# Gathers with their row numbers read in place: a grouped MoE kernel on one Trainium2 core

## Chip, cores and metric

One core of a Trainium2 chip. The metric is device time in microseconds (us), median of several runs; lower is better. TensorE is PE in the profile (its weight loads PEld), VectorE is DVE, ScalarE is ACT, GpSimd is POOL, and SyncE is SP. SP computes nothing here: it issues the plain DMAs. POOL issues the indirect ones.

## The reference

```python
# x: 64 x 64 x 512, so 4096 tokens of 512 values; 8 adapters of rank 16; 2 shared and 16 routed experts, 512 -> 256 -> 512
c = x @ W.T + scal[a] * ((x @ A[a].T) @ Bm[a].T)          # a: the adapter of each batch of 64 tokens
shared = sum_e gelu(c @ Wsh_up[e]) @ Wsh_down[e]
probs = softmax(c @ W_router); top_v, top_i = top_k(probs, 2)
routed = sum over the token's 2 experts of top_v * (gelu(c @ Wrt_up[e]) @ Wrt_down[e])
out = x + shared + routed
```

## The kernel before, in words

The tokens go in 16 chunks of 256, that is two tiles of 128 tokens each. There are four stages.

1. **Conditioning.** For each chunk PE computes `c` and the router's logits, SP stores `c` by rows in `xc_dram` and transposed in `xcT_dram`. DVE and ACT split the fp32 weights and activations into two fp16 halves.
2. **Early shared experts and sorting.** Chunks 0 to 5 go through the shared experts. DVE sorts the (token, expert) pairs into tiles of 128 rows of one expert each: `tok[:, j]` holds the token numbers of tile `j`, 79 tiles in all, and `pos[:, r, n]` holds, for the tokens of tile `n`, where their `r`-th routed row will lie. Both are finished once; the semaphore `sorted_ready` says so. While DVE sorts, POOL does some of the elementwise work of this stage: `add_x` (L537, the residual x of a chunk), `low_condT` (L542) and `low_hid` (L547, the low fp16 half of what `shared_down`, L1340, multiplies).
3. **Routed experts.** For each of the 79 tiles, POOL gathers 128 rows of `xc_dram` into one of two buffers `xg` (the function `gather`, L566), PE transposes them (`r_transpose_x`, L1377), multiplies up (L1393), transposes the middle (L1402) and multiplies down (L1412), and ACT scales the result into `rrow`, which SP stores in `r_dram`. A gather of tile `j` waits until PE has transposed tile `j - 2` (`xgT_psum`).
4. **The rest.** PE takes chunks 6 to 15 through the shared experts, `shared_up` (L1327) of one chunk ahead of `shared_down` (L1340) of the chunk before it. For all 16 chunks the routed rows are gathered back from `r_dram` (`gather_back`, L594), four indirect DMAs of 128 rows for each chunk, and DVE adds them, weighted by `gate`, onto the chunk's sum (`weigh`, L1168). I call these groups L6 to L15 for the chunks whose shared part is done in this stage, and E0 to E5 for the early chunks, whose sums were stored in `s_dram` and are loaded again. For L-chunks DVE then adds the shared part out of PE's bank (`add_shared`, L1193), and `shared_down` of the next chunk waits for that bank. SP loads x, the transposed `c` and the early sums, and stores the sums to `out`.

The order of each engine's queue is written out by hand. In stage 4 POOL's order of groups is L6 L7 E0 E1 L8 L9 E2 L10 E3 L11 E4 L12 E5 L13 L14 L15. There are four buffers of four tiles each (`slot`), so from L8 on a group first waits until DVE has weighed the group that had its buffer: L15 waits for E5 (`e_weighed`), for example. DVE's order for chunk c from 8 to 13 is `add_shared(c-1)`, `low_condT(c+2)` (L1123), weigh E(c-8), `low_hid(c+1)` (L1161), weigh L(c). PE's order is up(c+1), down(c), up(c+2), down(c+1), and so on.

In front of each gather (stage 3) and of each group of four (stage 4) POOL copies the row numbers out of `tok` or `pos` into a small tile, `slot_idx` (L571) or `row_idx` (L603), and waits for that copy's semaphore before it issues the indirect DMA (L574, L608). Most of both sequences are hardware loops (`pool.Fori`), so the column of `tok` or `pos` is a register there; the copy brings it to a fixed address.

Of the kernel before, what the change touches and what calls it, by code (L numbers as in the profile page):

```python
# [8 lines left out]
I32 = mybir.dt.int32  # L9
U32 = mybir.dt.uint32  # L10
# [5 lines left out]
P = 128  # L16
# [41 lines left out]
def adaln_moe_kernel(nc, xT, x_rows, idx, WT, AT, BmT, scal, sh_up, sh_dn, rt_w, w_r, out):  # L58
# [17 lines left out]
    with ctx:  # L76
        def sb(name, shape, dt=F32):
            return ctx.enter_context(nc.sbuf_tensor(name, shape, dt))

        def sem(name):  # L80
            return ctx.enter_context(nc.semaphore(name))
# [156 lines left out]
        def col(v, n):  # L238
            return v[:, n:n + 1]

        slot_idx = [sb(f"slot_idx{s}", [P, 1], I32) for s in range(2)]
        row_idx = [sb(f"row_idx{s}", [P, K_TOP, NT], I32) for s in range(4)]

        bank = [ctx.enter_context(nc.psum_tensor(f"bank{i}", [P, 512], F32)) for i in range(8)]
        XA, COND, XPOSE, LOGIT = bank[0], bank[1:3] + bank[6:8], bank[3:5], bank[5]
# [29 lines left out]
        up_ready, gelu_ready = sem("up_ready"), sem("gelu_ready")  # L275
        down_ready, shared_ready = sem("down_ready"), sem("shared_ready")
        x_loaded, sum_ready = sem("x_loaded"), sem("sum_ready")
        idx_first, idx_ready = sem("idx_first"), sem("idx_ready")
        xg_loaded = sems("xg_loaded")
        xgT_psum, xgT_ready = sem("xgT_psum"), sem("xgT_ready")  # L280
        r_up_ready, r_gelu_ready = sem("r_up_ready"), sem("r_gelu_ready")
        midT_psum, midT_ready = sem("midT_psum"), sem("midT_ready")
        r_dn_ready, rrow_ready = sem("r_dn_ready"), sem("rrow_ready")
        rrow_stored = sems("rrow_stored")
        c_idx_first, c_idx_ready, e_idx_first, e_idx_ready = (
            sem("c_idx_first"), sem("c_idx_ready"), sem("e_idx_first"), sem("e_idx_ready"))
        y_loaded, e_loaded, c_r_loaded = sems("y_loaded"), sems("e_loaded"), sems("c_r_loaded", 4)
        half_weighed, weighed, e_half_weighed, e_weighed = (
            sem("half_weighed"), sem("weighed"), sem("e_half_weighed"), sem("e_weighed"))
# [203 lines left out]
        @block.gpsimd  # L493
        def _(pool):
            def iota(dst, n):
                nc.gpsimd.iota(dst, [[1, n]], base=0, channel_multiplier=0,
                               allow_small_or_imprecise_dtypes=True).then_inc(iotas, 1)

            nc.gpsimd.iota(part_i[:], [[0, 1]], base=0, channel_multiplier=1).then_inc(iotas, 1)
            iota(iota_p[:], P)  # L500
            iota(iota_j[:], NJ_ALL)
            iota(iota_e[:], E_RT)
            nc.gpsimd.iota(tok_no[:], [[P, TT]], base=-TOK // 2, channel_multiplier=1,
                           allow_small_or_imprecise_dtypes=True).then_inc(iotas, 1)
            nc.gpsimd.memset(ident[:], 0.0).then_inc(masks, 1)
            nc.gpsimd.memset(ones[:], 1.0).then_inc(masks, 1)
            nc.gpsimd.memset(lower[:], 1.0).then_inc(masks, 1)
            pool.wait_ge(masks, 3)
            nc.gpsimd.affine_select(out=ident[:], in_=ident[:], compare_op=ALU.not_equal, fill=1.0, base=0,
                                    pattern=[[-1, P]], channel_multiplier=1).then_inc(consts, 1)  # L510
            nc.gpsimd.affine_select(out=lower[:], in_=lower[:], compare_op=ALU.is_gt, fill=0.0, base=0,
                                    pattern=[[1, P]], channel_multiplier=-1).then_inc(consts, 1)

            def reduce_max(n, a, b):

                pool.wait_ge(largest_ready, n)
                nc.gpsimd.partition_all_reduce(largest_all[:, a:b], largest[:, a:b], P, RMAX).then_inc(reduced, 1)

            def x_reduce(c, s):
                pool.wait_ge(x_max_ready, c - 1)
                nc.gpsimd.partition_all_reduce(x_max_all[s][:], x_max[s][:], P, RMAX).then_inc(x_reduced, 1)  # L523

            reduce_max(1, LIN_W, SH_UP)
            reduce_max(2, SH_UP, RT_UP)
            pool.wait_ge(scale_ready, 1)
            for c in range(2, NC):
                x_reduce(c, c % 2)
                if c == NC // 2 + 1:  # L530
                    reduce_max(3, RT_UP, C_ALL)

            def add_x(i, s):
                c = 2 * i + s
                pool.wait_ge(shared_ready, NT * c + NT)
                pool.wait_ge(x_loaded, 16 * (c + 1))
                nc.gpsimd.tensor_tensor(rows[s][:], rows[s][:], xres, ALU.add).then_inc(sum_ready, 1)  # L537


            def low_condT(c):  # L540
                pool.wait_ge(condT_half, c + 1)
                nc.gpsimd.tensor_tensor(actT[c % 2][:, 1], by_block(early_condT(c)), actT[c % 2][:, 0],  # L542
                                        ALU.subtract).then_inc(actT_ready, 1)

            def low_hid(c):
                pool.wait_ge(hid_half, c + 1)
                nc.gpsimd.tensor_tensor(hidT[c % 2][:, 1], by_block(tmp[:]), hidT[c % 2][:, 0],  # L547
                                        ALU.subtract).then_inc(hid_ready, 1)

            low_condT(0)  # L550
            low_condT(1)
            for c in range(EARLY - 2):
                low_hid(c)
                low_condT(c + 2)
                if c:
                    add_x((c - 1) // 2, (c - 1) % 2)
            low_hid(EARLY - 2)


            pool.wait_ge(sorted_ready, 1)  # L560
            for s in range(2):
                pool.wait_ge(rows_stored[s], 16 * A_HALF)

            def gather(i, s, first):  # L566
                j = 2 * i + s
                copied = idx_first if first else idx_ready
                if not first:
                    pool.wait_ge(xgT_psum, j - 1)  # L570
                nc.gpsimd.tensor_copy(slot_idx[s][:], tok[:, bass.ds(j, 1)]).then_inc(copied, 1)  # L571
                pool.wait_ge(sorted_ready, 1)
                pool.wait_ge(copied, j + 1 if first else j - 1)
                nc.gpsimd.indirect_dma_start(  # L574
                    out=xg[s], out_offset=None, in_=xc_dram,
                    in_offset=bass.IndirectOffsetOnAxis(ap=slot_idx[s][:].bitcast(U32), axis=0),
                ).then_inc(xg_loaded[s], 16)

            for s in range(2):
                gather(0, s, True)  # L580
            add_x((EARLY - 3) // 2, (EARLY - 3) % 2)
            low_hid(EARLY - 1)
            low_condT(EARLY)
            for s in range(2):
                gather(1, s, False)
            add_x((EARLY - 2) // 2, (EARLY - 2) % 2)
            for s in range(2):
                gather(2, s, False)
            add_x((EARLY - 1) // 2, (EARLY - 1) % 2)
            with pool.Fori(3, NJ_2) as i:  # L590
                for s in range(2):
                    gather(i, s, False)
            gather(NJ_2, 0, False)

            def gather_back(c, slot, n, first_copied, copied, used=None):
                if used is None:
                    copied, before = first_copied, n + 1
                else:  # L600
                    before = n - 1
                    pool.wait_ge(used, before)
                nc.gpsimd.tensor_copy(row_idx[slot][:], pos[:, :, bass.ds(c * NT, NT)]).then_inc(copied, 1)  # L603
                pool.wait_ge(sorted_ready, 1)
                pool.wait_ge(copied, before)
                for r in range(K_TOP):
                    for t in range(NT):
                        nc.gpsimd.indirect_dma_start(  # L608
                            out=routed_row(slot, r, t), out_offset=None, in_=r_dram,
                            in_offset=bass.IndirectOffsetOnAxis(ap=row_idx[slot][:, r, t:t + 1].bitcast(U32), axis=0),  # L610
                        ).then_inc(c_r_loaded[slot], 16)

            def gather_late(c, s, used=None):
                gather_back(c, s, c - EARLY, c_idx_first, c_idx_ready, used)

            def gather_early(k, s, used=None):
                gather_back(k, 2 + s, k, e_idx_first, e_idx_ready, used)

            pool.wait_ge(r_dn_ready, NJ)
            for s in range(2):  # L620
                pool.wait_ge(rrow_stored[s], 16 * (NJ_2 + 1 - s))
            for s in range(2):
                gather_late(EARLY + s, s)
            for s in range(2):
                gather_early(s, s)

            gather_late(EARLY + 2, 0, weighed)
            with pool.Fori(EARLY // 2 + 1, A_HALF - 2) as i:
                for s in range(2):
                    gather_late(2 * i + s + 1, 1 - s, weighed)  # L630
                    gather_early(2 * i + s - EARLY, s, e_weighed)
            gather_late(NC - 3, 1, weighed)
            for s in range(2):
                gather_back(NC - 2 + s, 2 + s, EARLY + s, e_idx_first, e_idx_ready, e_weighed)


        @block.scalar
# [869 lines left out]
```

## Time and profile before

| | before |
|---|---|
| median of 3 runs | 685.81 us (685.29 to 686.54) |
| profiled execution, span | 679.9 us |
| PE / DVE / ACT / POOL busy | 92% / 67% / 48% / 33% |
| indirect DMAs issued by POOL | 79 + 64 |
| HBM | 86.38 MB read, 49.02 MB written |

The profile gives the profiled execution by its span, from its first instruction to its last, 679.9 us. The runs are timed from outside; their median is 5.9 us more. POOL's busy share is low, but a share is an average over the four stages: the sequencer's own time, and waits, are in none of the percentages. A row of the timeline reads: start, duration, engine, line, operation, output from input, count, and in brackets how long the engine had been idle before it and what ended that.

### The profile page before, as it was taken

What the parts mean: (1) busy time and instruction counts of PE and PEld (TensorE: products, weight loads), DVE (VectorE), ACT (ScalarE), POOL (GpSimd) and SP (SyncE); (2) the same over time, 40 slices, a digit from 0 to 9 for tenths busy, and PEclk for the clock granted to TensorE, in tenths of its full rate; (3) what the DMA queues carried; (4) which work ended last, traced back from release to release, by engine and by line L of the source; (5) the groups of instructions that cost most, each with busy time, mean ns of one, the idle gap of its engine ahead of it and who ended that gap; (6) DMA issues with size and microseconds to landing.
All of it is one profiled execution on the core that took longest, in us unless ns stands there. A gap on an engine that the chain in (4) does not pass through costs nothing.

```text
span 679.9 us, 13742 instructions
## 1 busy us (share of the span) xinstructions
PE 627.5 (92%) x4115; PEld 428.4 (63%) x4117; DVE 457.4 (67%) x900; ACT 327.2 (48%) x480; POOL 222.6 (33%) x288
## 2 busy tenths in 40 slices
PE   4998999999989758889999999999999999989794
PEld 2465656566657435556777777777777777665561
DVE  2779999999974998525555555555555554688674
ACT  1333224677775743464555555555555554333230
POOL 1000000101012742373333333333333306777771
PEclk9997999999998988999999999999999999999898
DMA  7688994343334312165555555555555539989966
GB/s 275 281 312 286 374 346 168 123 157 142 132 127 128 124 63 93 32 217 171 159 159 169 161 154 159 164 168 157 156 159 167 164 107 377 366 301 362 369 205 248
DMA packets 49765, 135.68 MB, mean 200 GB/s; under 512 B 6160, under 2 KB 6288, under 8 KB 47312
## 3 DMA queue, kind: packets, MB, share of 16 engines
q1 hardware_dynamic: 38304, 97.93, 39.1%
q0 software_dynamic: 11440, 37.50, 20.0%
q8 instruction: 11, 0.18, 0.1%
q14 instruction: 10, 0.08, 0.0%
HBM read 86.38 MB, written 49.02 MB: 199 GB/s over the span
## 4 chain that ended last, share of the span: by engine, by line
PE 53%; DVE 17%; POOL 12%; issue 7%; DMA 7%; ACT 1%; SPq 0%; DVEq 0%; POOLq 0%; ACTq 0%
PE bank L1412 15%; PE bank L1393 14%; POOL rtw L608 9%; PE bank L1249 7%; PE bank L1377 5%; DVE lot_max L906 5%; DMA act_in<-xT 3%; PE bank L1402 2%; PE bank L1327 2%; PE bank L1257 2%; PE bank L1274 2%; DMA region<-xc_dram,slot_idx 2%; PE bank L1238 1%; DVE x_max L947 1%; PE bank L1265 1%
## 5 line engine op out<-in xcount | busy, mean ns | idle before, releaser
L1129 DVE SCALAR_TENSOR_TENSOR region<-bank,scale,region 128x512 f16<-128x512 f32 x79 | 59.2, 751 | 128.7 <-ACT region L809 128.7
L1393 PE MATMUL bank<-rtw,region 128*128 x948 | 116.4, 273 | 0.0
L1412 PE MATMUL bank<-rtw,tmp 128*128 x474 | 115.2, 379 | 0.6 <-DVE tmp L1137 0.6
L1393 PEld LDWEIGHTS bank<-rtw,region 128*128 128x128 f16 x948 | 92.8, 98 | 10.1
L1340 PE MATMUL bank<-shw,hid 128*128 128x512 f16 x384 | 91.3, 397 | 8.3 <-DVE rtw L1193 7.7
L574 POOL DMA_INDIRECT region<-xc_dram,slot_idx x79 | 77.1, 976 | 61.3 <-POOL slot_idx L571 61.3
L1327 PE MATMUL bank<-act_in,shw 128*128 128x256 f16 x768 | 89.4, 277 | 2.9 <-ACT tmp L756 1.7
L1327 PEld LDWEIGHTS bank<-act_in,shw 128*128 128x128 f16 x768 | 75.8, 100 | 16.0 <-ACT tmp L756 2.2
L816 ACT ACTIVATE region<-bank,un_dn 128x512 f32<-128x512 f32 x79 | 54.3, 687 | 57.3 <-PE bank L1412 54.8
L608 POOL DMA_INDIRECT rtw<-r_dram,row_idx x64 | 70.0, 1093 | 27.6 <-issue 14.8
L1340 PEld LDWEIGHTS bank<-shw,hid 128*128 128x128 f16 x384 | 38.4, 102 | 56.4 <-issue 10.0
L1412 PEld LDWEIGHTS bank<-rtw,tmp 128*128 128x128 f16 x474 | 46.3, 98 | 39.2 <-issue 1.3
L805 ACT ACTIVATE tmp<-bank,un_up 128x256 f32<-128x256 f32 x79 | 37.4, 473 | 60.2 <-PE bank L1393 60.2
L1168 DVE SCALAR_TENSOR_TENSOR rtw<-rtw,gate 128x512 f32 (+1 forms) x64 | 45.4, 750 | 15.2 <-DMA rtw<-r_dram,row_idx 13.0
L809 ACT ACTIVATE region<-bank,scale 128x512 f16<-128x512 f32 x79 | 54.1, 687 | 2.2 <-PE bank L1377 2.2
L523 POOL PARTITION_ALL_REDUCE x_max_all<-x_max x14 | 10.7, 763 | 134.9 <-DVE x_max L949 134.9
L1377 PE MATMUL bank<-ident,region 128*128 128x128 f32 x316 | 47.4, 273 | 2.6 <-DMA region<-xc_dram,slot_idx 2.5
L571 POOL COPY slot_idx<-tok 128x1 int32 (+1 forms) x79 | 14.4, 182 | 106.5 <-PE bank L1377 97.0
L756 ACT ACTIVATE tmp<-bank,un_up 128x256 f32<-128x256 f32 x44 | 20.4, 471 | 52.2 <-PE bank L1327 49.9
L641 ACT ACTIVATE rtw<-rtw,scale 128x1024 f16<-128x1024 f32 (+1 forms) x32 | 35.8, 1152 | 17.3 <-DVE rtw L935 15.1
L935 DVE SCALAR_TENSOR_TENSOR rtw<-rtw,scale 128x1024 f16<-128x1024 f32 x32 | 39.6, 1279 | 4.4 <-ACT rtw L641 4.3
L1135 DVE TENSOR_SCALAR tmp<-bank,to_mid 128x256 f16<-128x256 f32 x79 | 38.2, 484 | 6.1 <-PE bank L1402 2.7
(157 smaller groups left out, 910.0 us busy)
## 6 DMA issues: line engine op xcount, KB each, us to landing
r_dram<-region SPq DMA_DIRECT2D x79, 256.0 KB
rtw<-rt_w SPq DMA_DIRECT2D x16, 1024.0 KB, 7.4
act_in<-xT SPq DMA_DIRECT2D x16, 512.0 KB, 3.8
xc_dram<-rows SPq DMA_DIRECT2D x16, 512.0 KB, 3.7
xcT_dram<-hid SPq DMA_DIRECT2D x16, 512.0 KB, 2.8
rtw<-x_rows SPq DMA_DIRECT2D x16, 512.0 KB, 5.4
rtw<-xcT_dram SPq DMA_DIRECT2D x13, 512.0 KB, 6.1
out<-rtw SPq DMA_DIRECT2D x9, 512.0 KB, 5.6
```

The costliest lines, as they stand in the source:

```text
L574: nc.gpsimd.indirect_dma_start(out=xg[s], out_offset=None, in_=xc_dram, in_offset=bass.IndirectOffsetOnAxis(ap=slot_idx[s][:].bitcast(U32) ...
L608: nc.gpsimd.indirect_dma_start(out=routed_row(slot, r, t), out_offset=None, in_=r_dram, in_offset=bass.IndirectOffsetOnAxis(ap=row_idx[slo ...
L809: nc.scalar.activation(xgT[s][:, 0], R_XT[s][:].rearrange("p (k t) -> p k t", k=HK), ACT.Copy, scale=col(scale, C_ALL).bitcast(F32)).then_ ...
L816: nc.scalar.activation(rrow[s], R_DN[s][:], ACT.Copy, scale=col(un_dn, ROUTED)).then_inc(rrow_ready, 1)
L1129: nc.vector.scalar_tensor_tensor(xgT[s][:, 1], R_XT[s][:].rearrange("p (k t) -> p k t", k=HK), col(scale, C_ALL).bitcast(F32), xgT[s][:, 0 ...
L1168: last = nc.vector.scalar_tensor_tensor(y, routed_row(slot, r, t), gate[:, r, bass.ds(c * NT + t, 1)], y, ALU.mult, ALU.add)
L1249: last = mm(COND[NT * s + t][:], act_in[s][:, k, at] if whole else xp[s][:, ap, k, at], w_in[:, k, :] if whole else wt[:, bp, k, :], start ...
L1327: last = mm(UP[em % 2][:, 0:CHUNK], shw[:, e, w0:w0 + P], actT[s][:, xp, k, :], start=(k == 0 and n == 0), stop=(k == HK - 1 and n == 2))
L1340: last = mm(DOWN[t][:], hidT[s][:, xp, em, t * P:(t + 1) * P], shw[:, em // DM, w0:w0 + H], start=(em == 0 and n == 0), stop=(em == EM - 1 ...
L1377: last = nc.tensor.transpose(R_XT[s][:, k * P:(k + 1) * P], xg[s][:, k * P:(k + 1) * P], ident[:])
L1393: last = mm(R_UP[s][:, 0:D], xgT[s][:, xp, k, :], rtw[:, bass.ds(e, 1), w0:w0 + D].rearrange("p a d -> p (a d)"), start=(k == 0 and n == 0 ...
L1412: last = mm(R_DN[s][:], midT[s][:, xp, m, :], rtw[:, bass.ds(e, 1), w0:w0 + H].rearrange("p a h -> p (a h)"), start=(m == 0 and n == 0), s ...
```

## The change

The two index tiles and their copies go, with the waits on the copies and the six semaphores for them. Each indirect DMA takes its row numbers straight from a column of `tok` or `pos`. The loops of both sequences become Python loops, so that every column is a constant and all 79 + 64 indirect DMAs stand one by one in POOL's program. The waits on `xgT_psum`, `weighed` and `e_weighed` and the order of the DMAs stay.

```diff
-        slot_idx = [sb(f"slot_idx{s}", [P, 1], I32) for s in range(2)]
-        row_idx = [sb(f"row_idx{s}", [P, K_TOP, NT], I32) for s in range(4)]
...
-            def gather(i, s, first):
-                j = 2 * i + s
-                copied = idx_first if first else idx_ready
-                if not first:
+            def gather(j):
+                if j >= 2:
                     pool.wait_ge(xgT_psum, j - 1)
-                nc.gpsimd.tensor_copy(slot_idx[s][:], tok[:, bass.ds(j, 1)]).then_inc(copied, 1)
-                pool.wait_ge(sorted_ready, 1)
-                pool.wait_ge(copied, j + 1 if first else j - 1)
                 nc.gpsimd.indirect_dma_start(
-                    out=xg[s], out_offset=None, in_=xc_dram,
-                    in_offset=bass.IndirectOffsetOnAxis(ap=slot_idx[s][:].bitcast(U32), axis=0),
-                ).then_inc(xg_loaded[s], 16)
+                    out=xg[j % 2], out_offset=None, in_=xc_dram,
+                    in_offset=bass.IndirectOffsetOnAxis(ap=tok[:, j:j + 1].bitcast(U32), axis=0),
+                ).then_inc(xg_loaded[j % 2], 16)
...
-            with pool.Fori(3, NJ_2) as i:
-                for s in range(2):
-                    gather(i, s, False)
-            gather(NJ_2, 0, False)
+            for j in range(6, NJ):
+                gather(j)
...
-            def gather_back(c, slot, n, first_copied, copied, used=None):
-                if used is None:
-                    copied, before = first_copied, n + 1
-                else:
-                    before = n - 1
+            def gather_back(c, slot, used=None, before=0):
+                if used is not None:
                     pool.wait_ge(used, before)
-                nc.gpsimd.tensor_copy(row_idx[slot][:], pos[:, :, bass.ds(c * NT, NT)]).then_inc(copied, 1)
-                pool.wait_ge(sorted_ready, 1)
-                pool.wait_ge(copied, before)
                 for r in range(K_TOP):
                     for t in range(NT):
+                        n = c * NT + t
                         nc.gpsimd.indirect_dma_start(
                             out=routed_row(slot, r, t), out_offset=None, in_=r_dram,
-                            in_offset=bass.IndirectOffsetOnAxis(ap=row_idx[slot][:, r, t:t + 1].bitcast(U32), axis=0),
+                            in_offset=bass.IndirectOffsetOnAxis(ap=pos[:, r, n:n + 1].bitcast(U32), axis=0),
                         ).then_inc(c_r_loaded[slot], 16)
...
-            gather_late(EARLY + 2, 0, weighed)
-            with pool.Fori(EARLY // 2 + 1, A_HALF - 2) as i:
-                for s in range(2):
-                    gather_late(2 * i + s + 1, 1 - s, weighed)
-                    gather_early(2 * i + s - EARLY, s, e_weighed)
+            gather_back(EARLY + 2, 0, weighed, 1)
+            for k in range(2, EARLY):
+                gather_back(EARLY + k + 1, 1 - k % 2, weighed, k)
+                gather_back(k, 2 + k % 2, e_weighed, k - 1)
```

## Rows read from the trace of the kernel before

**Rows 1.** The page: shares by engine and by line of the chain that ended last.
```profile
PE 53%; DVE 17%; POOL 12%; issue 7%; DMA 7%; ACT 1%; SPq 0%; DVEq 0%; POOLq 0%; ACTq 0%
```

**Rows 2.** Busy time by stretch: us, PE, PEld, DVE, ACT, POOL, PEclk, DMA share, GB/s.
```profile
313.30:555.90 242.60, 242.59 (x1780) 181.63 (x1781) 127.73 (x222) 134.29 (x222) 81.83 (x142) 1.00 0.54 158
561.90:601.00 39.10, 37.35 (x272) 26.33 (x270) 22.81 (x28) 16.59 (x27) 28.01 (x32) 1.00 1.00 368
601.00:640.70 39.70, 35.22 (x227) 22.41 (x228) 32.19 (x42) 12.73 (x19) 29.21 (x31) 0.96 0.96 347
561.90:673.00 111.10, 102.33 (x680) 66.29 (x678) 76.67 (x96) 36.32 (x56) 75.47 (x80) 0.98 0.94 333
586.00:596.00 10.00, 10.00 (x70) 6.65 (x69) 6.16 (x8) 3.96 (x6) 7.19 (x9) 1.00 1.04 403
```

**Rows 3.** Groups of instructions by line on POOL: busy us, mean ns, idle before by releaser.
```profile
L608 POOL DMA_INDIRECT rtw<-r_dram,row_idx x64 | 70.0, 1093 | 27.6 <-issue 14.8 <-POOL row_idx L603 12.7
L603 POOL COPY row_idx<-pos 128x4 int32<-128x4 int32 (+1 forms) x16 | 5.5, 347 | 17.6 <-DMA r_dram<-region 17.6
```

**Rows 4.** Timeline of POOL in stage 4: the first group, the last, and one in the loop.
```profile
561.86 0.19 POOL L603 COPY row_idx<-pos 128x4 int32<-128x4 int32 x1 [17.56 <-DMA r_dram<-region]
562.85 0.97 POOL L608 DMA_INDIRECT rtw<-r_dram,row_idx  x1 [0.81 <-POOL row_idx L603]
...
567.01 0.95 POOL L608 DMA_INDIRECT rtw<-r_dram,row_idx  x1 [0.30 <-issue]
...
633.05 0.76 POOL L603 COPY row_idx<-pos 128x4 int32 x1
...
658.47 0.19 POOL L603 COPY row_idx<-pos 128x4 int32<-128x4 int32 x1
659.45 0.97 POOL L608 DMA_INDIRECT rtw<-r_dram,row_idx  x1 [0.79 <-POOL row_idx L603]
...
663.98 1.02 POOL L608 DMA_INDIRECT rtw<-r_dram,row_idx  x1 [0.30 <-issue]
```

**Rows 5.** Timeline of PE in stage 4: the five `shared_down` that waited.
```profile
601.77 5.35 PE L1340 MATMUL bank<-shw,hid 128*128 128x512 f16 x24 [2.52 <-DVE rtw L1193]
623.05 5.35 PE L1340 MATMUL bank<-shw,hid 128*128 128x512 f16 x24 [0.27 <-DVE rtw L1193]
637.09 7.04 PE L1340 MATMUL bank<-shw,hid 128*128 128x512 f16 x24 [3.44 <-DVE rtw L1193]
660.17 5.34 PE L1340 MATMUL bank<-shw,hid 128*128 128x512 f16 x24 [0.39 <-DVE rtw L1193]
666.56 5.34 PE L1340 MATMUL bank<-shw,hid 128*128 128x512 f16 x24 [1.05 <-DVE rtw L1193]
```

**Rows 6.** Timeline of DVE in stage 4: weighing E5, weighing L15, and the last `add_shared`.
```profile
653.71 1.42 DVE L1168 SCALAR_TENSOR_TENSOR rtw<-rtw,gate 128x512 f32 x2 [0.15 <-DVE rtw L1168]
...
673.08 2.87 DVE L1168 SCALAR_TENSOR_TENSOR rtw<-rtw,gate 128x512 f32<-128x512 f32 x4 [6.00 <-DMA rtw<-r_dram,row_idx]
675.98 1.41 DVE L1193 SCALAR_TENSOR_TENSOR rtw<-bank,un_dn,rtw 128x512 f32<-128x512 f32 x2
```

**Rows 7.** By tile: the indirect DMAs into the routed rows, from issue to landing.
```profile
DMA to landing us min/median/max: 3.3/6.2/9.0
```

**Rows 8.** Timeline of POOL where stage 3 begins.
```profile
282.16 0.19 POOL L571 COPY slot_idx<-tok 128x1 int32<-128x1 int32 x1 [9.48 <-DVE tok L1119]
283.31 1.30 POOL L574 DMA_INDIRECT region<-xc_dram,slot_idx  x1 [0.96 <-POOL slot_idx L571]
...
307.64 0.99 POOL L574 DMA_INDIRECT region<-xc_dram,slot_idx  x1 [0.77 <-POOL slot_idx L571]
```

**Rows 9.** Timeline of PE where stage 3 begins: its three waits for POOL's work.
```profile
291.11 5.35 PE L1340 MATMUL bank<-shw,hid 128*128 128x512 f16 x24 [0.61 <-POOL hid L547]
...
304.93 0.66 PE L1377 MATMUL bank<-ident,region 128*128 128x128 f32 x4 [0.81 <-DMA region<-xc_dram,slot_idx]
...
313.31 0.66 PE L1377 MATMUL bank<-ident,region 128*128 128x128 f32 x4 [1.65 <-DMA region<-xc_dram,slot_idx]
```

**Rows 10.** The page: DMA queues, those that fetch instructions (packets, MB, share).
```profile
q8 instruction: 11, 0.18, 0.1%
q14 instruction: 10, 0.08, 0.0%
```

More of the change, by code:

```diff
@@ L277, in adaln_moe_kernel @@
         x_loaded, sum_ready = sem("x_loaded"), sem("sum_ready")
-        idx_first, idx_ready = sem("idx_first"), sem("idx_ready")
         xg_loaded = sems("xg_loaded")
@@ L284, in adaln_moe_kernel @@
         rrow_stored = sems("rrow_stored")
-        c_idx_first, c_idx_ready, e_idx_first, e_idx_ready = (
-            sem("c_idx_first"), sem("c_idx_ready"), sem("e_idx_first"), sem("e_idx_ready"))
         y_loaded, e_loaded, c_r_loaded = sems("y_loaded"), sems("e_loaded"), sems("c_r_loaded", 4)
@@ L562, in _ @@
                 pool.wait_ge(rows_stored[s], 16 * A_HALF)
-            def gather(i, s, first):
-                j = 2 * i + s
-                copied = idx_first if first else idx_ready
-                if not first:
+            def gather(j):
+                if j >= 2:
                     pool.wait_ge(xgT_psum, j - 1)
-                nc.gpsimd.tensor_copy(slot_idx[s][:], tok[:, bass.ds(j, 1)]).then_inc(copied, 1)
-                pool.wait_ge(sorted_ready, 1)
-                pool.wait_ge(copied, j + 1 if first else j - 1)
                 nc.gpsimd.indirect_dma_start(
-                    out=xg[s], out_offset=None, in_=xc_dram,
-                    in_offset=bass.IndirectOffsetOnAxis(ap=slot_idx[s][:].bitcast(U32), axis=0),
-                ).then_inc(xg_loaded[s], 16)
-            for s in range(2):
-                gather(0, s, True)
+                    out=xg[j % 2], out_offset=None, in_=xc_dram,
+                    in_offset=bass.IndirectOffsetOnAxis(ap=tok[:, j:j + 1].bitcast(U32), axis=0),
+                ).then_inc(xg_loaded[j % 2], 16)
+            for j in range(2):
+                gather(j)
             add_x((EARLY - 3) // 2, (EARLY - 3) % 2)
@@ L583, in _ @@
             low_condT(EARLY)
-            for s in range(2):
-                gather(1, s, False)
+            for j in range(2, 4):
+                gather(j)
             add_x((EARLY - 2) // 2, (EARLY - 2) % 2)
-            for s in range(2):
-                gather(2, s, False)
+            for j in range(4, 6):
+                gather(j)
             add_x((EARLY - 1) // 2, (EARLY - 1) % 2)
-            with pool.Fori(3, NJ_2) as i:
-                for s in range(2):
-                    gather(i, s, False)
-            gather(NJ_2, 0, False)
-            def gather_back(c, slot, n, first_copied, copied, used=None):
-                if used is None:
-                    copied, before = first_copied, n + 1
-                else:
-                    before = n - 1
+            for j in range(6, NJ):
+                gather(j)
+            def gather_back(c, slot, used=None, before=0):
+                if used is not None:
                     pool.wait_ge(used, before)
-                nc.gpsimd.tensor_copy(row_idx[slot][:], pos[:, :, bass.ds(c * NT, NT)]).then_inc(copied, 1)
-                pool.wait_ge(sorted_ready, 1)
-                pool.wait_ge(copied, before)
                 for r in range(K_TOP):
                     for t in range(NT):
+                        n = c * NT + t
                         nc.gpsimd.indirect_dma_start(
                             out=routed_row(slot, r, t), out_offset=None, in_=r_dram,
-                            in_offset=bass.IndirectOffsetOnAxis(ap=row_idx[slot][:, r, t:t + 1].bitcast(U32), axis=0),
+                            in_offset=bass.IndirectOffsetOnAxis(ap=pos[:, r, n:n + 1].bitcast(U32), axis=0),
                         ).then_inc(c_r_loaded[slot], 16)
[L613 to L617, printed above, removed]
             pool.wait_ge(r_dn_ready, NJ)
@@ L622, in _ @@
             for s in range(2):
-                gather_late(EARLY + s, s)
-            for s in range(2):
-                gather_early(s, s)
-            gather_late(EARLY + 2, 0, weighed)
-            with pool.Fori(EARLY // 2 + 1, A_HALF - 2) as i:
-                for s in range(2):
-                    gather_late(2 * i + s + 1, 1 - s, weighed)
-                    gather_early(2 * i + s - EARLY, s, e_weighed)
-            gather_late(NC - 3, 1, weighed)
-            for s in range(2):
-                gather_back(NC - 2 + s, 2 + s, EARLY + s, e_idx_first, e_idx_ready, e_weighed)
+                gather_back(EARLY + s, s)
+            for k in range(2):
+                gather_back(k, 2 + k)
+            gather_back(EARLY + 2, 0, weighed, 1)
+            for k in range(2, EARLY):
+                gather_back(EARLY + k + 1, 1 - k % 2, weighed, k)
+                gather_back(k, 2 + k % 2, e_weighed, k - 1)
+            gather_back(NC - 3, 1, weighed, LATE - 4)
+            for s in range(2):
+                gather_back(NC - 2 + s, 2 + s, e_weighed, EARLY + s - 1)
         @block.scalar
```

## The prediction, made before the changed kernel was run

> **What bounds the kernel now.** I began with the chain that ended last. PE holds half of it, but POOL holds 12% and "issue" another 7% [rows 1], though POOL is busy for a third of the span only. So there is a stretch where POOL leads, and the view by stretches shows which. In stage 3 PE is busy for 242.59 of 242.60 us [rows 2]: nothing that POOL does there can matter unless it becomes late. In stage 4 (from 561.9) PE loses time, and the timeline of POOL says why: from 561.86 to 665.0 POOL issues its 64 gathers one behind the other, never waiting for a buffer, and all that separates them is 0.30 us of issue inside a group, and a copy and 0.79 us between groups [rows 3, 4]. At 599, 634 and 666 PE waits for a DVE that waits for a group of gathers [rows 5], and the last wait is the largest: the last gather lands at 673.0, DVE has been idle for 6.00 us, and the program ends 6.9 us later, after the weighing, the last add and the last store [rows 6]. So the end is set by POOL's queue. Close behind it stand PE, and the DMA engines: their busy share is 1.00 until 601 and 0.96 until 640.7 [rows 2].
>
> **The sum.** It is made against the span, 679.9 us; the runs' median is 5.9 us above that, and I take this difference as fixed.
>
> *POOL in stage 4.* Sixteen copies go: 5.5 us. Their sixteen waits, 12.7 us, go too [rows 3]. In place of them stands the gap between two gathers, 0.30 us each (14.8 us over 48 [rows 3]) before 15 of the 16 groups: 4.6 us. Net 5.5 + 12.7 - 4.6 = 13.6 us. The lower bound: most copies take 0.19 us, some up to 0.87 (the one at 633.05 took 0.76 [rows 4]), in stretches where DVE is at work; if that excess, 5.5 - 16 x 0.19 = 2.5 us, moves into the gathers that take the copies' places, 11.1 us are left. I take 13.6, since nothing shows the gathers being longer behind a copy than behind a gather. That a gather reads its numbers from `pos` or `tok` and not from a small tile I cost at nothing: each partition reads one number either way. That it stands in the open and not in a loop, nothing either: the gap is 0.30 in front of the loop and in its rows alike.
>
> *What is late next.* The last gather would land at 673.0 - 13.6 = 659.4 by POOL alone. Three others have a say.
>
> First, buffers. POOL has never waited for one, but the last group stands behind E5's weighing, which ends at 655.1 [rows 6], only 3.3 us before the group starts at 658.47 [rows 4]. E5's weighing moves with PE and DVE. What PE lost up to there is 2.52 + 0.27 + 3.44 and the 1.7 us by which the down at 637.09 took 7.04 instead of 5.34, when the granted clock had fallen behind the 3.44 us wait: 7.9 us [rows 5]. So E5 is done at 647.2, the group starts then, its last gather is issued 4.5 us after its first (659.45 to 663.98), and with the 9.0 us that this gather took to land [rows 7] it is there at 660.8; with the median of 6.2, at 658.
>
> Second, PE. Its waits in stage 4 come to 2.52 + 0.27 + 3.44 + 1.7 + 0.39 + 1.05 = 9.4 us [rows 5], so without them its last product is done at 671.9 - 9.4 = 662.5. One add (0.7) and the 2.5 us from DVE's last instruction to the end put the end no earlier than about 665.7, 14.2 us before now.
>
> Third, transfers. From 561.9 to 673.0 the core moved 333 GB/s x 111.1 us = 37.0 MB, and all of these bytes still move. While the DMA engines were always busy, the rate was 368 GB/s over 39 us, 347 at a share of 0.96, and 403 in the best ten microseconds [rows 2]. At 368 the 37.0 MB take 100.5 us: the last gather lands at 662.4. The shorter stretch stands nearer to the one at 1.00 than to a burst, so I take this rate.
>
> The latest of 659.4, 660.8 and 662.4 counts: 662.4, a gain of **10.6 us** in stage 4. Bounds: 13.6 at most (POOL), and 4.4 if the rate is 347 (106.7 us, landing at 668.6).
>
> Here the Trainium skill has a figure that speaks against the change. The page "DMA: Bandwidth & Descriptors", section "Specifications", gives about 358 GB/s as one core's limit at HBM. By it, an estimate, the 37.0 MB would take 103.4 us and the gain in stage 4 would be 7.7 us. The rows of 368 GB/s over 39 us and of 403 over ten are both above it, and the sum above does not use it.
>
> *Where stage 3 begins.* POOL's two first gathers stand behind a copy each, and behind them its own adds, which PE waits for. The first copy with its wait is 0.19 + 0.96 us, the second 0.2 + 0.8 less a gap of 0.3 [rows 8]: 1.8 us earlier, enough for PE's wait of 0.61 us on L547. Gathers of tiles 4 and 6 shed their own copies (0.18 + 0.77 each) on top of that and of the four in front, so they start 2 to 3.5 us earlier; PE's waits for them are 0.81 and 1.65 us [rows 9]. Sum 0.61 + 0.81 + 1.65 = **3.1 us**. Bound from below 1 us, if the load of x that the `add_x` at 304.4 waited for does not come earlier. PE then runs without a gap to 556, so this gain is carried whole.
>
> *Inside stage 3.* Seventy more copies go, with 0.18 + 0.77 us each, but PE is busy without a gap [rows 2]: its transposes have the tile in time and get it 0.95 us sooner. Worth nothing; PE's work is the cover. If PE were ever to wait there, the gain would be a gain in addition.
>
> Total 10.6 + 3.1 = 13.7 us, so 685.8 - 13.7 = **672.1 us**, of its own range 668.5 to 675.
>
> **The rivals.**
>
> *The transfers hold.* Gathers issued earlier wait in the DMA engines. For it: share 1.00 and 0.96 until 640.7, and gathers that take 6.2 us in the median against 3.3 at best [rows 2, 7]. Against it: 403 GB/s were reached, and the share falls to 0.94 over the whole stretch. At 347 GB/s stage 4 gives 4.4 us, stage 3 its 3.1: 678.3 us. Chance 0.25.
>
> *The gap is not the copy's.* A group that begins with a wait for a buffer (12 of 16) may pay the 0.79 us for waiting on a semaphore, whoever releases it, long satisfied or not. Against: the copies follow the gather before them without any gap although they carry such a wait. It would keep 12 x 0.49 = 5.9 us: POOL's gain 7.7, landing at 665.3, and with 2.6 at stage 3: 675.5 us. Chance 0.12.
>
> *Slower: the program is fetched.* POOL's program was short, with two loops; now 143 gathers stand in a row, and its instructions come by DMA, 0.18 MB in 11 packets so far, 16 KB each [rows 10]. In stage 4 such a fetch must share saturated engines; at the slowest landing seen, 9.0 us [rows 7], two fetches that POOL stands still for cost 18 us and outweigh the 13.7: 685.8 + 4.3 = 690.1 us. It decides from the second uncovered fetch on (13.7 / 9.0 = 1.5). Against: the straight part of the old program, 561.9 to 588, shows no such stop. Chance 0.04.
>
> *No difference:* the transfers fix the end and the x load fixes the start. 685.8 us, chance 0.03.
>
> The page "Runtime: NRT & Kernel Launch" of the Trainium skill, section "Instruction fetch mechanics", says that straight code is fetched ahead while it runs and that taken branches are what breaks this. That speaks against this rival, and no row here shows a fetch on the path.
>
> **How the numbers follow.** The forecast has 0.56. A measurement of this kernel can tell about 0.2%, 1.4 us, from no change. Faster by more: 0.56 + 0.25 + 0.12 = 0.93; the same 0.03; slower 0.04. The range runs from 668.5, the forecast with the last gather at 659.4 and a little beyond, to 680, which takes in the first two rivals.
>
> **What would show it.** POOL's groups at intervals of 4 x (1.09 + 0.30) = 5.6 us instead of 6.4, no row of L571 or L603; the first row of a group 0.30 us behind the last of the one before; a wait for DVE in front of the last group; the last landing near 659, which is 662.4 less stage 3's 3.1, on the span's clock; PE's waits in stage 4 under 3 us; 365 GB/s or more from 561 on; PE's three waits at the start of stage 3 gone. It is wrong if gathers take a median of 8 us or more to land (transfers), if 0.79 stays in front of groups, or if POOL stands still inside a group.

## The result, and the profile after

The changed kernel takes 702.77 us (median of 4 runs, 699.26 to 709.2) against 686.17 us for the kernel before (685.29 to 687.32) in the same set of runs: 1.0268 times as long [1.0215, 1.0321]. So it is slower by 2.7%, where 2% less was forecast. The profiled execution has a span of 698.0 us, against 679.9.

The lines of the changed kernel have other numbers. Its `shared_up` is L1302, `shared_down` L1315, `add_shared` L1168, `weigh` L1143 and the gather of a routed row L590; L731 is ACT's read of a bank of `shared_up`, L742 ACT's step behind four such reads.

The page of the changed kernel: what answers to [rows 1, 3, 10].

```profile
span 698.0 us, 13352 instructions
...
PE 632.2 (91%) x4115; PEld 429.7 (62%) x4117; DVE 457.6 (66%) x900; ACT 326.6 (47%) x480; POOL 200.9 (29%) x193
...
PEclk9998999999999798999999999999999997998999
...
q8 instruction: 11, 0.18, 0.1%
q14 instruction: 11, 0.09, 0.0%
...
PE 64%; DVE 18%; another core or an unknown queue 6%; DMA 4%; issue 3%; ACT 2%; POOL 1%; SPq 0%; DVEq 0%; ACTq 0%
...
L590 POOL DMA_INDIRECT rtw<-r_dram,pos x64 | 69.9, 1093 | 75.8 <-DVE rtw L1143 38.1
```

POOL's own work is as forecast: it is off the chain (12% before, 1% now) and the copies are gone. But its gathers wait 38.1 us for DVE, which they never did before; one such wait had been forecast, in front of the last group. And 6% of the chain has a name that was not in it, "another core or an unknown queue". Its place is stage 4. These are the changed kernel's stretches there, columns as in [rows 2].

```profile
558.30:597.00 38.70, 25.42 (x160) 16.36 (x159) 12.86 (x15) 9.33 (x14) 20.83 (x20) 0.87 0.80 288
597.00:636.00 39.00, 28.13 (x181) 18.15 (x180) 20.43 (x27) 9.25 (x15) 20.98 (x20) 0.90 0.82 292
```

PE was busy for 37.35 of 39.10 us here; now it is for 25.42 of 38.70, at a lower granted clock, and the DMA engines have time left (0.80). Nobody is at its limit. POOL's timeline of the changed kernel, stage 4:

```profile
584.04 0.94 POOL L590 DMA_INDIRECT rtw<-r_dram,pos  x1 [0.30 <-issue]
597.64 0.94 POOL L590 DMA_INDIRECT rtw<-r_dram,pos  x1 [12.65 <-DVE rtw L1143]
...
609.42 1.75 POOL L590 DMA_INDIRECT rtw<-r_dram,pos  x1 [7.08 <-DVE rtw L1143]
...
642.42 1.75 POOL L590 DMA_INDIRECT rtw<-r_dram,pos  x1 [11.23 <-DVE rtw L1143]
...
679.19 1.75 POOL L590 DMA_INDIRECT rtw<-r_dram,pos  x1 [7.10 <-DVE rtw L1143]
```

The first 20 gathers stand in an unbroken row, 0.30 us apart. From there on POOL waits four times for a buffer that DVE has not weighed. DVE waits for PE's products, and PE stands still too. What PE stands still for shows in two timelines of the changed kernel, ACT's and PE's.

```profile
567.15 1.14 ACT L742 ACTIVATE hid<-rtw,to_mid 128x1024 f16<-128x1024 f32 x1
580.22 0.47 ACT L731 ACTIVATE tmp<-bank,un_up 128x256 f32<-128x256 f32 x1 [11.93 <-remote]
587.26 0.84 ACT L731 ACTIVATE tmp<-bank,un_up 128x256 f32<-128x256 f32 x2 [6.57 <-remote]
...
625.98 0.47 ACT L731 ACTIVATE rtw<-bank,un_up 128x256 f32<-128x256 f32 x1 [11.60 <-remote]
633.12 0.84 ACT L731 ACTIVATE rtw<-bank,un_up 128x256 f32<-128x256 f32 x2 [6.66 <-remote]
```

```profile
568.99 2.78 PE L1302 MATMUL bank<-act_in,shw 128*128 128x256 f16 x24
580.75 2.74 PE L1302 MATMUL bank<-act_in,shw 128*128 128x256 f16 x12 [8.97 <-issue]
587.79 2.74 PE L1302 MATMUL bank<-act_in,shw 128*128 128x256 f16 x12 [4.31 <-ACT tmp L731]
```

Each read of a bank by ACT (L731) needs 12 matmuls of PE. By 571.8 PE had done 24, so two banks were ready, and PE waited until one was read. ACT waits for PE's signal and begins at 580.22, 8.5 us after both products were there. PE has one bank back at 580.7 and starts at once. ACT reads the second bank, also full since 571.8, only at 587.26, 15.5 us later, and in the program nothing stands between the two reads but the wait for PE's next signal. I read this as a signal that comes late: ACT waits for no data, PE for no work, and the profile finds no sender for what ends ACT's wait ("remote", though one core runs). The signal itself is in no view, so this is a reading and not a measurement. After the stops of 8.97 and 4.31 us twelve matmuls take 2.74 us, where 24 took 2.78: PE's clock had fallen from its upper to its lower level.

The waits of ACT from 556 on, changed kernel (us in all, times, longest):

```profile
ACT rtw L731 <- remote: 23.2, 4, 11.6
ACT tmp L731 <- remote: 21.0, 3, 11.9
```

In a trace of the same kernel without such waits (set B, below), the first two of the four reads wait 4.00 and 0.78 us, and later pairs 3.9 to 4.4 and 0.84. The four therefore hold 7.9 + 5.8 + 7.4 + 5.8 = 27 us too many, of the 34 us by which stage 4 is longer here than there (139.6 against 105.5). I put the rest down to the lower clock and some smaller waits, without having added them up.

### The profile page after: what moved, and what is told of

It reads as the page before. It is cut to its first block, busy times and chain, and to the rows that moved or that the text cites. A ratio compares the mean times of both kernels' runs of the same rounds, so it can differ in the third digit from the quotient of the medians.

```text
span 698.0 us, 13352 instructions
## 1 busy us (share of the span) xinstructions
PE 632.2 (91%) x4115; PEld 429.7 (62%) x4117; DVE 457.6 (66%) x900; ACT 326.6 (47%) x480; POOL 200.9 (29%) x193
## 4 chain that ended last, share of the span: by engine, by line
PE 64%; DVE 18%; another core or an unknown queue 6%; DMA 4%; issue 3%; ACT 2%; POOL 1%; SPq 0%; DVEq 0%; ACTq 0%
PE bank L1387 15%; PE bank L1368 15%; PE bank L1302 9%; PE bank L1224 7%; PE bank L1315 5%; PE bank L1352 5%; DVE lot_max L881 4%; DMA act_in<-xT 3%; PE bank L1377 2%; PE bank L1232 2%; PE bank L1249 2%; PE bank L1213 1%; DVE x_max L922 1%; DMA region<-w_r 1%
## 5 line engine op out<-in xcount | busy, mean ns | idle before, releaser
L564 POOL DMA_INDIRECT region<-xc_dram,tok x79 | 75.0, 950 | 177.9 <-PE bank L1352 169.6
L1302 PE MATMUL bank<-act_in,shw 128*128 128x256 f16 x768 | 96.4, 288 | 24.8 <-issue 11.7
L1302 PEld LDWEIGHTS bank<-act_in,shw 128*128 128x128 f16 x768 | 77.9, 103 | 42.7 <-issue 13.9
L1315 PE MATMUL bank<-shw,hid 128*128 128x512 f16 x384 | 90.7, 395 | 5.5 <-DVE rtw L1168 5.4
L590 POOL DMA_INDIRECT rtw<-r_dram,pos x64 | 69.9, 1093 | 75.8 <-DVE rtw L1143 38.1
L1315 PEld LDWEIGHTS bank<-shw,hid 128*128 128x128 f16 x384 | 38.5, 102 | 53.0 <-issue 10.4
L731 ACT ACTIVATE tmp<-bank,un_up 128x256 f32<-128x256 f32 x44 | 20.3, 472 | 74.8 <-PE bank L1302 46.8
L1143 DVE SCALAR_TENSOR_TENSOR rtw<-rtw,gate 128x512 f32 (+1 forms) x64 | 45.2, 747 | 2.0 <-DVE rtw L1143 1.7
L1098 DVE SCALAR_TENSOR_TENSOR act_in<-rtw,scale,act_in 128x1024 f16<-128x1024 f32 x9 | 11.6, 1283 | 48.4 <-ACT act_in L637 48.4
```

The source lines that it names most:

```text
L564: nc.gpsimd.indirect_dma_start(out=xg[j % 2], out_offset=None, in_=xc_dram, in_offset=bass.IndirectOffsetOnAxis(ap=tok[:, j:j + 1].bitcast ...
L590: nc.gpsimd.indirect_dma_start(out=routed_row(slot, r, t), out_offset=None, in_=r_dram, in_offset=bass.IndirectOffsetOnAxis(ap=pos[:, r, n ...
L1143: last = nc.vector.scalar_tensor_tensor(y, routed_row(slot, r, t), gate[:, r, bass.ds(c * NT + t, 1)], y, ALU.mult, ALU.add)
L1302: last = mm(UP[em % 2][:, 0:CHUNK], shw[:, e, w0:w0 + P], actT[s][:, xp, k, :], start=(k == 0 and n == 0), stop=(k == HK - 1 and n == 2))
L1315: last = mm(DOWN[t][:], hidT[s][:, xp, em, t * P:(t + 1) * P], shw[:, em // DM, w0:w0 + H], start=(em == 0 and n == 0), stop=(em == EM - 1 ...
```

## The experiments

Six sets of kernels ran, A to F, each on one chip, and each with its own runs of the kernel before. That kernel took 681 to 685 us (medians) in all of them, and every ratio is against the kernel before of its set.

**Set A: the parts.** The first kernel has the change in stage 3 alone, the second in stage 4 alone. The third keeps both copies, written out one by one, with one wait behind each instead of two. The fourth is the changed kernel with a copy and its wait in front of each group, into a tile that nobody reads.

```diff
 # e3 and e4: in front of each group of four (e3 also one in front of each gather of stage 3, and it reads from the copies)
+                nc.gpsimd.tensor_copy(row_idx[slot][:], pos[:, :, c * NT:(c + 1) * NT]).then_inc(c_idx_ready, 1)
+                pool.wait_ge(c_idx_ready, groups[0])
```

> Stage 3's gathers as in the changed kernel (one by one, in place), stage 4 as before. All three theories put the loss in stage 4; the trace after shows stage 3 begin 3.4 us earlier. Burst theory (64 gathers of stage 4 without a pause make PE's signals reach ACT and DVE late): about 682.5 us, since the 3.4 us of stage 3 stay. Source theory (reading row numbers in place out of a wide tile is what hurts): stage 3 reads in place too, but at wide intervals; 682 to 686. Program theory (143 gathers in a row lead to instruction fetches that stop an engine): 79 of them are here, so stage 4's stalls should be here in part, 686 to 695.

> Stage 3 as before, stage 4's gathers as in the changed kernel. Burst theory and source theory: the whole loss is here, 686.2 + (702.8 - 686.2) + 3.4 = about 706 us, between 700 and 712, with ACT waiting 8 to 12 us for signals of PE that are already done. Program theory: only 64 of the 143 are in the open; less than 700.

> Everything unrolled as in the changed kernel, but each gather and each group keeps its copy, its wait, and reads from the copy. Burst theory: the pause of 1 us between groups is back, 685 to 687 us. Source theory: nothing is read in place, 685 to 687. Program theory: the straight program is all here and longer, so it is as slow as the changed kernel, 699 or more.

> The changed kernel, with a copy of four columns of pos and the wait for it put back before each group of stage 4, into a tile that nobody reads; the gathers still read pos in place. Burst theory: the pause is back, so the stalls are gone, 682 to 684 us, stage 3's gain kept. Source theory: the row numbers are still read in place, so 700 or more. Program theory: 700 or more.

Measured: 0.9938 [0.9903, 0.9972], 0.9819 [0.9768, 0.987], 0.9871 [0.9832, 0.991] and 0.9852 [0.9822, 0.9883]. None was slower, although each of the three theories had put at least one of these kernels at 699 us or above, and the two halves of the change made 4.2 and 12.3 us of gain, against 3.1 and 10.6 forecast. The third kernel's timeline on POOL:

```profile
564.98 0.19 POOL L597 COPY row_idx<-pos 128x4 int32<-128x4 int32 x1
565.44 0.97 POOL L602 DMA_INDIRECT rtw<-r_dram,row_idx  x1 [0.27 <-POOL row_idx L597]
```

A copy with one wait costs 0.27 us of gap, not 0.79 [rows 4]. The other 0.5 us belonged to the second wait, on `sorted_ready`, which had been satisfied since before stage 3. That the gathers of stage 4 read in place (e4) or from the copy (e3) shows no difference beyond the intervals here, where no signal was late.

**Set B: the changed kernel again.** Since no part was slow, the whole had to be run again, and beside it with the six semaphores and the index tiles still allocated, unused, so that every other semaphore has the number it had before.

> The changed kernel itself, unaltered, a second time, beside the kernel before on one chip. In the runs so far each half of the change alone was faster than the kernel before (0.994 and 0.982), and so was the whole with an idle copy in each group (0.985). Theory of the pause (only the 64 gathers of stage 4 without a stop, together with stage 3's, hold PE's signals up): it is slow again, about 1.027 of before, with waits of ACT over 6 us. Theory of the place (the stalls belonged to the chip or the moment of the first runs, not to the program): it is as fast as the sum that was forecast, 0.978 to 0.985 of before, and ACT has no wait for late signals of PE.

> The changed kernel, with the six semaphores and the index tiles of the kernel before still allocated and used by nobody, so that every semaphore has the number that it had before. All the fast kernels so far kept them. Theory of the numbers (which semaphore the DMAs count on matters): fast here, 0.98 of before, while the unaltered changed kernel beside it is slow, 1.02 or more. Pause theory: both slow. Place theory: both fast and equal within 0.5%.

Measured: 0.9723 [0.9678, 0.9768] and 0.9764 [0.9721, 0.9806]. The unaltered changed kernel took 665.26 us (662.89 to 667.01). It is the program of the result above, 37.5 us away. Its page:

```profile
span 665.2 us, 13353 instructions
...
PE 66%; DVE 20%; DMA 6%; issue 3%; ACT 2%; SPq 1%; POOL 1%; DVEq 0%; ACTq 0%
...
L590 POOL DMA_INDIRECT rtw<-r_dram,pos x64 | 68.4, 1068 | 42.3 <-DMA r_dram<-region 19.0
```

Its stretches in stage 4:

```profile
558.00:597.00 39.00, 38.73 (x284) 27.46 (x282) 23.75 (x29) 15.86 (x26) 28.40 (x28) 1.00 1.02 386
597.00:636.00 39.00, 38.63 (x259) 24.80 (x257) 34.11 (x44) 14.36 (x21) 30.47 (x29) 1.00 1.01 375
```

Its timelines, of PE (all the waits of `shared_down` in stage 4), POOL, DVE and ACT:

```profile
596.67 5.35 PE L1315 MATMUL bank<-shw,hid 128*128 128x512 f16 x24 [0.27 <-DVE rtw L1168]
628.83 5.35 PE L1315 MATMUL bank<-shw,hid 128*128 128x512 f16 x24 [0.28 <-DVE rtw L1168]
650.19 5.34 PE L1315 MATMUL bank<-shw,hid 128*128 128x512 f16 x24 [0.34 <-DVE rtw L1168]
656.63 5.34 PE L1315 MATMUL bank<-shw,hid 128*128 128x512 f16 x24 [1.10 <-DVE rtw L1168]
...
645.44 1.75 POOL L590 DMA_INDIRECT rtw<-r_dram,pos  x1 [3.71 <-DVE rtw L1143]
...
650.38 0.95 POOL L590 DMA_INDIRECT rtw<-r_dram,pos  x1 [0.30 <-issue]
...
657.06 2.86 DVE L1143 SCALAR_TENSOR_TENSOR rtw<-rtw,gate 128x512 f32<-128x512 f32 x4
...
662.01 0.75 DVE L1168 SCALAR_TENSOR_TENSOR rtw<-bank,un_dn,rtw 128x512 f32<-128x512 f32 x1 [1.31 <-PE bank L1315]
...
571.73 0.47 ACT L731 ACTIVATE tmp<-bank,un_up 128x256 f32<-128x256 f32 x1 [4.00 <-PE bank L1302]
572.98 0.47 ACT L731 ACTIVATE tmp<-bank,un_up 128x256 f32<-128x256 f32 x1 [0.78 <-PE bank L1302]
```

This is close to the forecast's picture: PE waits 2.0 us in all and the last group waits for E5's buffer. The last group of gathers is weighed without a wait, and PE's last product sets the end: DVE's last add waits 1.31 us for it. No wait in stage 4 has "remote" behind it. The two rows of ACT are the first two reads that waited 11.93 and 6.57 us above.

**Set C: the changed kernel a third time.**

> The changed kernel a third time, unaltered, in more rounds. Place theory (the program is faster, about 0.975 of before, and the first measurement's stalls came from where or when it ran): 0.970 to 0.980 again. Theory of a rare stall (the program itself brings it on, now and then): some of the runs here are 690 us or more, beside others near 665. Pause theory: it fell with the second measurement, 0.972, and would need 1.02 here.

Measured: 1.0278 [1.0235, 1.032], 704.54 us, with waits for "remote" of up to 11.6 us in its trace, and POOL waiting at the same four places (12.92, 7.10, 11.24, 7.12 us). So both outcomes come back, each steady within its set. I call a set *prompt* when the signals come at once, and *late* when they don't. The kernel before without the copy's second wait, loops and copies kept, was planned with this set and gave no result.

**Set D: repeats, to find what the parts do in a late set.** It turned out prompt.

> The changed kernel a fourth time, as the yardstick of this job's chip. It has come out at 1.027 and 1.028 of before on one occasion each and at 0.972 on another, each time steady over its 4 to 6 runs; the slow ones lose their time in the same two places, where ACT waits for PE's signals. Chip theory: 0.97 or 1.03 here, nothing between, depending on the chip.

> Stage 3 as before (loops, copies), stage 4 as in the changed kernel. If this job's chip is one where the changed kernel is slow: theory that the 64 gathers of stage 4 in an unbroken row bring the stalls says 1.02 or more here too; theory that they come from stage 3 (its records of signals are already incomplete there) says 0.98. If the chip is a fast one: 0.98 by both.

> The changed kernel with an idle copy and its wait before each group of stage 4. On a chip where the changed kernel is slow: pause theory says fast, 0.985; stage 3 theory says slow, 1.02. On a fast chip: 0.985 by both.

> The changed kernel with the old semaphores still allocated, so that each has its old number. On a chip where the changed kernel is slow: theory of the numbers says fast, 0.976; the others say slow, 1.027. On a fast chip: 0.976 by all.

Measured: 0.975 [0.9665, 0.9834], 0.982 [0.9732, 0.9909], 0.9804 [0.9715, 0.9893] and 0.9748 [0.9652, 0.9844], in this order. The numbers of the semaphores make no difference in a prompt set; in a late one that kernel never ran.

**Set E: once more, with a kernel between.** The idle copy stands in front of every second group only.

```diff
+                if groups[0] % 2 == 0:
+                    nc.gpsimd.tensor_copy(row_idx[slot][:], pos[:, :, c * NT:(c + 1) * NT]).then_inc(c_idx_ready, 1)
+                    pool.wait_ge(c_idx_ready, groups[0] // 2)
```

> The changed kernel a fifth time, the yardstick of this job's chip. Chip theory: 0.975 or 1.028 of before, nothing between (so far 1.027 and 1.028 in two jobs, 0.972 and 0.975 in two others, which ran on one and the same chip).

> Stage 4 alone as in the changed kernel. On a chip where the changed kernel is slow: 1.03 by the theory that the unbroken gathers of stage 4 bring the stalls, 0.982 by the theory that the straight stage 3 does. On a fast chip 0.982 by both.

> The changed kernel with an idle copy and its wait before each group of stage 4. On a chip where the changed kernel is slow: 0.983 by the pause theory, 1.02 or more by the theory of stage 3. On a fast chip 0.983 by both.

> As the one above with the idle copy before every other group only. On a fast chip: between the changed kernel and the one with all copies, 0.978. On a slow chip, pause theory: if signals fall behind within a group or two, stalls as in the changed kernel, 1.01 to 1.03; if they need a longer row, 0.98.

Prompt again: 0.9737 [0.9715, 0.9759], 0.9796 [0.9773, 0.9819], 0.9811 [0.9784, 0.9837] and 0.9807 [0.9788, 0.9826]. The idle copy costs 0.7% (0.9811 against 0.9737, 5 us). Half as many copies cost as much within the intervals, where half the cost would have been 0.9774. The pages of the three kernels, in the order changed, copy everywhere, copy in every second group, show where it goes:

```profile
L590 POOL DMA_INDIRECT rtw<-r_dram,pos x64 | 68.4, 1068 | 42.3 <-DMA r_dram<-region 19.0
L600 POOL DMA_INDIRECT rtw<-r_dram,pos x64 | 72.4, 1131 | 19.2 <-issue 14.6
L601 POOL DMA_INDIRECT rtw<-r_dram,pos x64 | 74.7, 1168 | 37.9 <-DMA r_dram<-region 18.9
```

The gathers themselves take longer beside the copies, 4.0 and 6.3 us in all. From the first gather or copy to the last gather's start POOL needs 90.8 us in the changed kernel, 96.5 with all copies and 95.0 with half of them. The last group is weighed without a wait in the first, after 1.07 us of waiting for its gathers in the second and after 2.91 in the third. So the cost lies in POOL's queue again. Why the gathers take longer there was not tested.

**Set F: a late one at last.** With the changed kernel ran the change in stage 4 alone, and e3 with the second wait put back.

```diff
 # e19: e3, in both stages
+                pool.wait_ge(sorted_ready, 1)
                 pool.wait_ge(c_idx_ready, groups[0])
```

> The changed kernel a sixth time, the yardstick of this job's chip: 0.974 or 1.028 of before, nothing between.

> Stage 4 alone as in the changed kernel. On a chip where the changed kernel is slow: 1.03 if the unbroken gathers of stage 4 bring the stalls, 0.981 if stage 3 does. On a fast chip 0.981 by both.

> Unrolled, with copies, reading from them, as in the earlier kernel that came to 0.987, and with the second wait (on sorted_ready) between copy and gather put back. Theory that this wait is the half microsecond: the gap from copy to gather goes from 0.27 to 0.77 us, and the time back up by about 8 us, to 0.997 to 1.00 of before. Theory that the loop's registers cost it: the gap stays 0.27 and the time 0.987. On a slow chip the gap tells, whatever the time.

Measured: 1.0239 [1.018, 1.0298], 1.0316 [1.0239, 1.0393] and 0.9995 [0.9961, 1.0029]. The second is the kernel that made 0.982, 0.982 and 0.980 in sets A, D and E. Its ACT in stage 4, in the late set:

```profile
583.82 0.47 ACT L744 ACTIVATE tmp<-bank,un_up 128x256 f32<-128x256 f32 x1 [11.98 <-remote]
590.89 0.84 ACT L744 ACTIVATE tmp<-bank,un_up 128x256 f32<-128x256 f32 x2 [6.59 <-remote]
```

and the first of the two in the trace of set E:

```profile
573.14 0.47 ACT L744 ACTIVATE tmp<-bank,un_up 128x256 f32<-128x256 f32 x1 [4.00 <-PE bank L1315]
```

So neither the new stage 3 nor the missing semaphores and tiles are needed for the loss (this kernel still allocates all of them): the new gathers of stage 4 are enough. The third kernel (e19) has both stages written out one by one too, but keeps the copies with the pause behind them and reads its row numbers from them, and it loses nothing. POOL's timeline, and the waits of ACT:

```profile
568.32 0.20 POOL L598 COPY row_idx<-pos 128x4 int32<-128x4 int32 x1
569.31 0.97 POOL L604 DMA_INDIRECT rtw<-r_dram,row_idx  x1 [0.79 <-POOL row_idx L598]
```

```profile
ACT tmp L745 <- remote: 9.9, 4, 3.9
ACT rtw L745 <- remote: 9.9, 2, 5.0
```

The gap of 0.79 us is back with the second wait alone, which settles what it was made of: 0.27 for the copy's signal and 0.5 for the second wait. The late signals are there too, 19.8 us in six waits, but none is longer than 5.0 us, where the changed kernel's reach 11.9. So the late signals belong to the set, and how much they cost to the kernel: this one loses nothing that is seen against the kernel before. Two things set its stage 4 apart from the kernel that lost 3% beside it, 1 us between groups and row numbers read from a small tile, and no late set has them one at a time.

## Why the prediction was wrong

**Stage 4 on POOL** held everywhere. No row of a copy is left, the first row of a group stands 0.30 us behind the last of the one before it, and a wait for DVE stands in front of the last group. Gathers are no longer than before (1068 and 1093 ns against 1093 [rows 3]), so the excess of the copies did not move into them.

**What is late next** is the step that failed. It named buffers, PE and transfers as the only others that have a say. In the prompt sets that was right, but the wrong one of them was taken: transfers did not decide, since 386 and 375 GB/s were reached where 368 was taken, and stage 4 took 105.5 us against 118.0, a gain of 12.5 where 10.6 was forecast. POOL waits there for a buffer (the 3.71 us in front of the last group), but its gathers are in time, and PE sets the end. In the late sets a fourth thing decides, the time between PE's product and the moment at which ACT and DVE go on with it: 8.5 and 15.5 us at the first stop, 27 us too many over four waits, and stage 4 takes 139.6 us. The sum has no term for it and so put it at nothing; [rows 2 to 5] show PE busy or waiting for something with a name, and gave no sign of it.

**Stage 3** began as forecast: 3.1 us were expected, the trace of set B has none of the three waits [rows 9] and one of 0.60 us for DVE became 0.26, 3.4 in all, and stage 3's half alone gave 4.2 +/- 2.3 us. Stage 4 begins 2.2 us earlier in that trace (559.66 against 561.86); what comes ahead of stage 3 differs too from trace to trace. *Inside stage 3* nothing more came.

**The whole** in the prompt sets: 0.972 to 0.975, that is 17 to 19 us, against 13.7. The end of the trace was forecast at 679.9 - 13.7 = 666.2 us, and came at 665.2. That it fits so well is partly luck. The 5.9 us between the span and the median were taken as fixed, but the runs of the kernel before lie only 2.0 us above their own spans (1.7 to 1.8 for the changed kernel), so the profiled execution was some 4 us faster than the median one, and the gain against medians is larger than the one against that trace. In the late sets: 1.024 to 1.028.

**The rivals.** *Transfers hold*: no, by the rates above. *The gap is not the copy's*: half right. Most of the 0.79 us was indeed a wait's price and not the copy's, but of a second wait behind the copy; with the buffer's wait alone in front of it (12 groups of 16), a group starts 0.30 us behind the one before. *The program is fetched* was the only rival that ended slower, and its 690.1 lay nearest to what came, but its mechanism is not what happened. POOL never stops inside a group, and 143 gathers in a row brought one packet more (q14 has 11 where it had 10). Nor was it another engine's program: q8 and q14 hold 22 packets, and between 580 and 597, and between 614 and 626, where ACT stood still for 6.6 and 11.6 us, none of them ran. The three packets near the first stop, between 568 and 578, ran between 568 and 576 in the prompt trace of set B too, and stopped nobody; one more ran at 628 to 630, inside the fourth stop, and its like in set B, at 612 to 614, stopped nobody either.

**What stays open.** Nothing in the traces tells what differs between a prompt and a late set. It isn't the program, and not the chip's number, since sets B, D and F carry the same one. It lasts through a set. The kernel before shows little of it: its medians are 683.3 to 686.2 us in the late sets and 681.1 to 683.8 in the prompt ones. Its only trace has no wait for "remote", but no run says in which kind of set it was taken. Why it is spared is argued and not shown. It would fit that pauses let signals through: in e19 the waits are short, and in the changed kernel long ones begin inside unbroken rows of gathers (558 to 585, 609 to 631). It would fit as well that it and e19 read their row numbers from a small tile and the two kernels that lose read them out of `pos`. The kernel that could tell the two apart is e4, which pauses and reads in place, and it never met a late set; in prompt sets the place makes no difference. How an unbroken row of indirect DMAs would delay PE's signals was not seen. The profiler's own records could have a part in what is printed as "remote", and in the loss itself, since every run on record carries a span and a granted clock. Whether one pause of 0.5 us is enough (e3, e4) could not be seen either.

## What to carry to other kernels

Look for satisfied waits: a second wait between a copy and its indirect DMA cost 0.5 us each time. The kernel written out with its copies and without that wait gained 1.3%, of the 2.7% to be had in a prompt set, and with the wait nothing (0.9995, though in a late set). And a change like this one is to be run in several sets before it is kept: one set of runs, however tight its interval, showed either -2.7% or +2.7% here. When an engine waits for a product that PE finished long ago, look at when it was told, since no sum over busy times will show it.

## What the runs showed of the hardware

- **One program, two times.** The changed kernel stood at 1.027, 1.028 and 1.024 in three sets and at 0.972, 0.975 and 0.974 in three others, with nothing between.
- **Late signals.** ACT read one bank 8.5 us and the next 15.5 us after PE had filled them. What follows from it came back in almost the same size in each late trace of the changed kernel and of its stage 4 alone, four in all: POOL's first wait for DVE was 12.65, 12.92, 12.7 and 12.7 us, its second 7.1 and its third 11.2 us each time.
- **A second wait has a price on POOL.** Copy to indirect DMA: 0.27 us with one wait, 0.79 us with a second, satisfied one.
- **The transfer rate.** 386 GB/s over 39 us is above what the Trainium skill gives as one core's limit at HBM (page "DMA: Bandwidth & Descriptors", section "Specifications", about 358 GB/s). That row gets its figure by dividing a stack's 716 GB/s by two cores, and here one core ran the program. As a cap for a lone core the trace does not agree with it, and the measurement decides.
